# One signal per multiplied chunk instead of one per row block, and one signal less in the first layer

## The reference

```python
h = relu(layernorm(x));  x = x + L0(h)   # sum of h[src] * edge_weight by dst, divided by the degree, two linear maps
h = relu(layernorm(x));  x = x + L1(h)   # attention: w1[dst] - w2[src] + d, a softmax per dst, sum of a * (w3[src] + d)
h = relu(layernorm(x));  x = x + L2(h)   # silu(batchnorm([h[src], edge_attr_64] @ W1 + b1)), mean by dst, a second MLP
h = relu(layernorm(x));  x = x + L3(h)   # sum of h[src] by dst
```

## Time and profile before

| | us |
|---|---|
| time, median of 3 runs | 2036.69 (2029.17 to 2037.15) |
| span of the profiled execution | 2601.9 |
| PE busy (matmuls) | 1601.6 (62%) |
| VectorE busy | 1551.6 (60%) |
| ScalarE busy | 895.7 (34%) |
| GpSimd busy | 1327.9 (51%) |

### The profile page before, as it was taken

The page is one execution under the profiler, slowest core; times in us unless marked ns, Lnnn a source line. Parts: engine busy times, 40 slices in busy tenths (PEclk is TensorE's granted clock), DMA queues, the critical chain, the costliest instruction groups (busy, mean ns, idle before and its releaser), DMA issues.

```text
span 2601.9 us, 23168 instructions
## 1 busy us (share of the span) xinstructions
PE 1601.6 (62%) x6953; PEld 1209.1 (46%) x6953; DVE 1551.6 (60%) x2430; ACT 895.7 (34%) x1175; POOL 1327.9 (51%) x1397
## 2 busy tenths in 40 slices
PE   1546554555565655555665247888786725889892
PEld 1334433443354444444453235666565514767672
DVE  5445545554477477677776635554555934868783
ACT  1222222222231755555553113332333811433340
POOL 6555555455534455555664455446551036656554
PEclk8566666666676777787787568898897657989896
DMA  6111211121121344444444313323224602333332
GB/s 141 36 51 54 63 52 51 53 63 52 52 68 54 99 142 145 139 141 147 145 146 129 83 37 70 69 59 75 65 65 101 204 13 53 85 78 84 78 79 57
DMA packets 223807, 219.66 MB, mean 84 GB/s; under 512 B 108066, under 2 KB 170967, under 8 KB 223447
## 3 DMA queue, kind: packets, MB, share of 16 engines
q1 hardware_dynamic: 175575, 147.75, 19.3%
q0 software_dynamic: 44384, 56.98, 10.5%
q10 hardware_dynamic: 3744, 13.63, 1.3%
HBM read 116.77 MB, written 101.46 MB: 84 GB/s over the span
## 4 chain that ended last, share of the span: by engine, by line
PE 23%; another core or an unknown queue 13%; issue 11%; DVE 11%; ACT 5%; POOL 3%; DMA 2%; SPq 1%; DVEq 0%; POOLq 0%; ACTq 0%
PE psum L993 16%; POOL arena L676 3%; PE psum L1018 1%; DVE scan_ring L1935 1%; DVE spare L1935 1%; DMA maxima<-arena 1%; DVE arena L1810 1%; PE psum L1085 1%; ACT spare L1257 1%; DVE arena L1816 1%; PE psum L1024 1%; ACT spare L1331 1%; DMA keep<-keep_rows 1%; DVE spare L1760 1%
## 5 line engine op out<-in xcount | busy, mean ns | idle before, releaser
L636 POOL DMA_INDIRECT gathered<-table,idx x1264 | 1208.6, 956 | 1014.9 <-issue 363.6
L1760 DVE COPY_PREDICATED spare<-spare,psum 64x512 f32<-64x512 uint8 x300 | 220.8, 736 | 303.7 <-ACT spare L1355 208.2
L993 PE MATMUL psum<-rounded 128*128 128x512 f32 x1144 | 303.8, 419 | 63.8 <-issue 43.4
L993 PEld LDWEIGHTS psum<-rounded 128*128 128x128 f32 x1144 | 227.3, 202 | 124.9 <-issue 59.2
L780 PE MATMUL psum<-ident,arena 128*128 128x128 f32 x416 | 107.9, 409 | 287.5 <-ACT arena L1140 272.1
L1592 DVE TENSOR_REDUCE rs<-arena 128x16 f32<-128x1024 f32 x52 | 63.4, 1219 | 302.3 <-ACT arena L1144 249.6
L780 PEld LDWEIGHTS psum<-ident,arena 128*128 128x128 f32 x416 | 69.8, 205 | 354.9 <-ACT arena L1140 284.0
L1144 ACT ACTIVATE arena<-psum 128x1024 f32<-128x1024 f32 x52 | 53.3, 1025 | 410.9 <-remote 280.3
L1355 ACT ACTIVATE spare<-psum 64x512 f32<-64x512 f32 x82 | 48.5, 592 | 397.7 <-remote 199.0
L676 POOL DMA_INDIRECT arena<-scan,rowidx x75 | 79.3, 1058 | 206.7 <-DMA scan<-ea 114.3
L906 PE MATMUL psum<-ident,arena 128*128 128x128 f32 x172 | 34.4, 335 | 189.3 <-ACT arena L1246 185.5
(11 more groups left out here) (285 smaller groups left out, 3444.9 us busy)
## 6 DMA issues: line engine op xcount, KB each, us to landing
scan<-ostage SPq DMA_DIRECT2D x130, 256.0 KB, 2.3
scan<-arena SPq DMA_DIRECT2D x52, 512.0 KB
gathered<-table,idx POOLq DMA_INDIRECT x1264
d_mlp<-arena ACTq DMA_DIRECT2D x26, 512.0 KB
arena<-d_mlp SPq DMA_DIRECT2D x52, 256.0 KB
maxima<-arena SPq DMA_DIRECT2D x52, 256.0 KB
ea<-in_edge_attr SPq DMA_DIRECT2D x104, 128.0 KB
spare<-src_row SPq DMA_DIRECT2D x100, 128.0 KB
```

The costliest lines, as they stand in the source:

```text
L636: pool.indirect_dma_start(out=out[:, j, hf, :], out_offset=None, in_=tab[layer], in_offset=bass.IndirectOffsetOnAxis(ap=idx[:, j, hf * NCH ...
L993: last = nc.tensor.matmul(P[:, bank + t, :], parts[layer][n][:, b:b + 2, :].rearrange("p b d -> p (b d)"), tile(layer, m, u)[:, hf * CH:(h ...
L1760: picked = v.copy_predicated(rows[m % 2][halves[hf], :], quarter[m % 2][halves[hf], q - 1, :], P[halves[q % 2], bank + q // 2, :])
```

## The change

TensorE raises `L1 onehots used`, `L2 onehots used` and `L3 onehots used` only after the last block of a chunk's second half, by 7 at once. The thresholds of those who wait are as they were. In layer 0 the semaphore `hist added` is gone; VectorE waits for `out transposed [0]` instead, which TensorE raises behind the same iteration's count.

```diff
-            for name in ("hist added", "gelu made", "norms2 made"):
+            for name in ("gelu made", "norms2 made"):
...
             def l0_hist(i):
-                    last = nc.tensor.matmul(P[:, 7, 0:NB], one_p[0:HR, t * 128:(t + 1) * 128],
+                    nc.tensor.matmul(P[:, 7, 0:NB], one_p[0:HR, t * 128:(t + 1) * 128],
...
-                last.then_inc(S("hist added"), 1)
...
             def l1_multiply(m, hf, blocks):
-                    if hf == 1:
-                        last.then_inc(S("L1 onehots used"), 1)
+                    if hf == 1 and u == NU - 1:
+                        last.then_inc(S("L1 onehots used"), NU)
...
             def multiply(layer, m, hf, bank):
-                    if hf == 1:
-                        last.then_inc(S(f"L{layer} onehots used"), 1)
+                    if hf == 1 and u == NU - 1:
+                        last.then_inc(S(f"L{layer} onehots used"), NU)
...
             def count(i):
-                dve.wait_ge(S("hist added"), past(i))
+                dve.wait_ge(S("out transposed", 0), n_out_transposed(0, i))
...
-            dve.wait_ge(S("hist added"), past(NIT))
+            dve.wait_ge(S("out transposed", 0), n_out_transposed(0, NIT))
```

## The result

The changed kernel takes 2088.81 us (median of 4 runs, 2083.98 to 2089.31), the kernel before 2036.47 us beside it (4 runs, 2029.17 to 2037.15): a ratio of 1.0264, 95% interval 1.0237 to 1.029. It is 52 us slower, as forecast.

What follows compares the result with a forecast made beforehand. The prediction took GpSimd's almost never waiting gathers to bound the kernel, with layer 2's loop ending alongside them. Terms 48 + 3 + 0 + 1 + 0 = 52 us on 2036.7 gave 2089 us, range 2056 to 2110.

Steps and rivals of the forecast that it cites:

- 48 + 3 + 0 + 1 + 0: Added us: layer 2's waits 48, layer 1 3, layer 3 0, layer 0 1, increments left out 0.
- all four signs: ScalarE's unbroken 3.35 us chain in 18 places, VectorE starting there too, GpSimd's L1024 waits 2.7 us longer, layer 3 unchanged.
- both kinds cost 2.74 us: Layer 2: steps with two fetched chunks between and with one each lengthen by 2.74 us, 18 times, 49 us.
- the clock: Rival: added pauses bring TensorE's lower clock in one of four layer 2 halves, 57 us on top, 2146 us; chance 0.08.
- the pauses are short beside the idle times of the first profile: Against the lower clock: TensorE's added pauses are 2.7 us, beside existing idle times of 5 us and more.
- the gathers cover 1 us: Layer 2: gathers (334 us) and loop (335.5 us) end together, so gathers hide only 1 us of the added 49.
- 5 us for landing and the last chunk: Layer 2's end: some 5 us added to the gathers' 329.2 us, giving 334 us.
- Increments: TensorE: 326 increments left out give 0 us, 1 us at most; rival that they were dear, 2028 us, chance 0.03.
- its forecast of 1 us: Layer 0's end: the copy of the counts waits for four more transposes, 1 us, between 0 and 3.
- the forecast of 3 us: Layer 1: seven added waits for block 3's one-hot, mostly covered, cost 3 us, between 0 and 25.
- partial cover: Layer 2: unprofiled loop 20 us faster, so gathers hide part, 2066 us; chance 0.17 together with half-free steps.

Runs made afterwards that it cites:

- l2_only: The kernel before with one signal per chunk in layer 2 alone, layers 0, 1 and 3 as before: 2086.55 us, ratio 1.0253.
- act_whole3: The kernel before with only ScalarE's one-hots of layer 2 waiting for the whole chunk: 2084.3 us against 2027.75, ratio 1.0282.
- two_sig3: The kernel before with two signals per second half in layer 2, behind blocks 2 and 6: 2029.03 us against 2027.75, ratio 1.0009.
- the long execution: The kernel before, unchanged, in its first profile: span 2601.9 us, against a median of 2036.69 us.
- rounded_waits: The kernel before, signals per block kept, but waiting one-hots of layers 1 to 3 round thresholds up to a whole chunk: 2086.98 us, ratio 1.0248.
- all_but_l2: The whole change except in layer 2, which signals per block as in the kernel before: 2040.72 us, ratio 1.002.

## Why the prediction came true, and where its terms were off

**The sum, 52 us, and what it consists of.** Of the terms 48 + 3 + 0 + 1 + 0, the first is the whole effect (`l2_only` 50). Its mechanism is as foretold, and all four signs of it came: the three operations in 18 places, VectorE's start at the same time, GpSimd's waits on TensorE, layer 3 as before. That the number fits to the microsecond is luck, because two errors cancel: the loop grew by 58 us and not 49, and 10 us of that were covered and not 1. It is luck in the measurement too, since beside the changed kernel three of the four runs of the kernel before are near 2037 us and one at 2029.17; on a chip where most are near 2028, the same wait costs 57 us (`act_whole3`).

**The step "both kinds cost 2.74 us" failed in both kinds.** From the copies in the trace after: 3.2 us from the first gather to the first copy; 8.1 us in the first two steps together; then 11 steps with two fetched chunks at 20.08 instead of 17.74, 2.34 us each, 25.8 us; 4 steps with one fetched chunk at 21.73 instead of 16.38, 5.35 us each, 21.4 us; and -0.4 in the last step, whose own copy has no one-hots in front. Sum 58.

With two fetched chunks, 0.4 of the 2.74 us is hidden. The prediction passed them on in full, but the copy that TensorE waits for had some slack before: it ended at 1328.91 (L1362 at 1328.31), 0.54 us ahead of the product that reads it (L1018 at 1329.45). After, it is the last to come: it ends at 1323.67 and the product starts at 1323.72. `two_sig3` shows the same 0.4 us: 0.47 went in and 0.06 came out. With one fetched chunk the mechanism was named rightly (TensorE is held at block 4, by `pick` behind the late copy), but not its consequence. TensorE after:

```profile
1343.85 1.09 PE L992 MATMUL psum<-rounded_spare,rounded_keep 128*128 128x512 f32 x4
1348.27 2.08 PE L992 MATMUL psum<-rounded_spare,rounded_keep 128*128 128x512 f32 x4 [3.33 <-DVE rounded_spare L1771]
1350.14 1.91 PE L992 MATMUL psum<-rounded_ea,rounded_keep 128*128 128x512 f32 x4
1351.85 1.06 PE L992 MATMUL psum<-rounded_ostage,rounded_keep 128*128 128x512 f32 x2
1352.70 1.06 PE L1006 MATMUL psum<-ident,ea 128*128 128x128 f32 x4
```

The same step before:

```profile
1317.06 1.20 PE L993 MATMUL psum<-rounded_spare,rounded_keep 128*128 128x512 f32 x4 [0.58 <-DVE rounded_spare L1772]
1318.10 1.08 PE L993 MATMUL psum<-rounded_ea,rounded_keep 128*128 128x512 f32 x4
1319.02 0.63 PE L993 MATMUL psum<-rounded_ostage,rounded_keep 128*128 128x512 f32 x2
1319.48 0.60 PE L1007 MATMUL psum<-ident,ea 128*128 128x128 f32 x4
```

The wait is 3.33 instead of 0.58 us: 2.75, the 2.74 of the sum. But behind it the ten matmuls take 4.43 us instead of 2.42 (1348.27 to 1352.70, 1317.06 to 1319.48), and the transposes and product 0.6 us more. The windows of this stretch after say why (length, busy of PE, PEld, DVE, ACT and POOL with counts, granted clock, DMA share, GB/s):

```profile
1341.00:1345.00 4.00, 3.94 (x19) 2.92 (x17) 3.60 (x7) 3.24 (x5) 3.08 (x4) 1.00 0.14 25
1345.00:1348.00 3.00, 0.00 (x0) 0.00 (x0) 2.86 (x4) 0.00 (x0) 2.09 (x4) 0.86 0.29 79
1348.00:1354.00 6.00, 5.73 (x15) 4.59 (x16) 2.33 (x6) 0.80 (x2) 2.76 (x3) 0.50 0.52 112
1354.00:1357.00 3.00, 3.00 (x13) 2.16 (x12) 1.90 (x3) 2.12 (x3) 0.00 (x0) 1.00 0.33 77
```

TensorE stood from 1344.9 to 1348.3, and the 6 us behind that ran at a granted clock of 0.50, its lower level of 1.2 GHz. Before, the same stretch is at 1.00 throughout. The changed kernel has five such pauses of 3.3 us, one in each step with one fetched chunk. Behind four of them TensorE runs for about 6 us at the lower level, which costs 2.6 us each; behind the first it does so for 3 us, and once more for 3 us behind a pause of 2.09 us in the next step, together 3.1 us. So the rival "the clock" came true in small: some 13.5 of the loop's 58 us, not the 57 of its price.

`l2_only` separates the two parts. There the pause of 3.33 us that ends at 1259.08 is followed by a granted clock of 1.00 (six microseconds from 1259 on), and the step is 19.11 us: 2.73 more than before, the forecast's price without the clock. The lower level came there behind the next pause, of 2.09 us (1.58 us more in that step). Of the 13 pauses of 2.09 us in each kernel, one in the changed kernel and two in `l2_only` were followed by the lower level; no row says which pause brings it. The sentence that the pauses are short beside the idle times of the first profile was the error; that profile's idle times belonged to the long execution.

**The step "the gathers cover 1 us" was off by 9.** The loop's end was near the forecast (338.1 us after the first gather where no gather is late, forecast 335.5). GpSimd's last issue ended at 335.0 us, 6 later than the 329.2 of the sum, and the "5 us for landing and the last chunk" were 11.8 (346.8 - 335.0). That SP's masks are issued ahead of the last gather stood in no row that I had read. Where the gather isn't late, the change should cost the whole 58 us: beside `act_whole3`, where 16 of 17 runs of the kernel before lie below 2034, the cost was 57.

**Increments.** 0 was right. The Trainium skill ("TensorE: Matmul & The Clock Gate", The cost: per-tile semaphore tail) puts 26.3 ns on each for packed matmuls, which would have been an estimated 8.6 us. The runs here don't show it for matmuls of 128x512 one behind the other: `rounded_waits`, with the increments of layers 1 to 3 kept, is not slower than the changed kernel, and the halves of the earlier trace rows said so beforehand.

**Layers 0, 1 and 3.** Layer 3 is unchanged (+0.3 us) and layer 0 ends 0.4 us earlier, so its forecast of 1 us isn't seen. For layer 1 the forecast of 3 us is neither shown nor refuted: it lasts 489.2 us after and 487.2 in `all_but_l2`, against 486.1 before and 483.1 in `l2_only`, and two profiles of the same layer differ by as much as the effect. `all_but_l2`'s 4 us has an interval from -1 to 9.

**The range.** Its lower end came from partial cover, which does exist (10 of 58 us), its upper end from the clock, which also came (13.5 us). They moved the time by about as much in opposite directions, and neither took it out of the range.

## What to carry to other kernels

Before a signal is made coarser, list for each waiter which block it waits for and what is queued behind it on its engine: here seven signals were worth 50 us, two placed near the blocks that someone waits for were as good as seven, and no cost of an increment showed. A wait put in 18 times must be read in each kind of step, and a pause of TensorE can cost more than its length, by the slower clock behind it (2.75 + 2.6 us in four steps, 2.73 alone in one). Here a profile whose span was far from the runs could still carry a sum, once the waits that it added were taken out; the second profile of the same kernel settled it.

## What the runs showed of the hardware

- A pause of TensorE of 3.33 us was followed by some 6 us at a granted clock of 0.50 (the 1.2 GHz level) in four steps of the changed kernel and by 3 us of it in a fifth; in one step of `l2_only` the same pause was followed by none. One of 13 pauses of 2.09 us in the changed kernel and two of 13 in `l2_only` were followed by 3 us of it.
- Four transfers that SP issued at 1501.69 came with a gather issued at 1503.24 for which TensorE stood 9.16 us (9.14 in `all_but_l2`); with the transfers behind the gather the wait was 0.93 us, or none (`two_sig3`).
- In executions of about 2.6 ms an added wait costs a third or less, as a ratio, of what it costs in ordinary ones (0.45% against 2.8% for ScalarE's alone, 0.42% against 1.4% for VectorE's): they are no place to measure an edit.
